# Sums of a state-space scan spread over seven slots of eight, with filler products on TensorE

## The reference

```python
def step(h, inputs):
    d_t, B_t, C_t, u_t = inputs
    dA = jnp.exp(d_t[:, :, None] * A)
    h = h * dA + (d_t * u_t)[:, :, None] * B_t[:, None, :]
    y_t = jnp.einsum('bdn,bn->bd', h, C_t)
    return (h, y_t)
...
_, ys = jax.lax.scan(step, h0, seq)
y = jnp.transpose(ys, (1, 0, 2)) + u * D
y = y * jax.nn.silu(z)
out = y @ W_out
return residual + out
```

## Time and profile before

| | |
|---|---|
| median of 3 runs | 1419.47 us (1418.7 to 1422.88) |
| profiled execution, its own time | 1428.01 us |
| its span | 1426.0 us |
| first scan starts, last scan ends | 80.7 us, 416.2 us |
| PE, DVE, ACT, POOL busy, share of the span | 78%, 60%, 37%, 40% |
| granted TensorE clock, mean over the span | 0.813 |

### The profile page before, as it was taken

How to read it: one execution, slowest core, us unless ns; L and a number is a source line. 1 busy time by engine, 2 the same in 40 slices (tenths; PEclk the granted TensorE clock), 3 DMA queues, 4 the chain that set the end, 5 groups by cost and what they waited for, 6 DMA issues and landing times. The chain is left out here.

```text
span 1426.0 us, 29397 instructions
## 1 busy us (share of the span) xinstructions
PE 1109.9 (78%) x11843; PEld 810.9 (57%) x11843; DVE 849.1 (60%) x1500; ACT 529.4 (37%) x1322; POOL 569.8 (40%) x382
## 2 busy tenths in 40 slices
PE   3478999989987989897455598599376999856795
PEld 1167888888873544555345255445365454543595
DVE  7576888888855674466512476557413486755233
ACT  2433444444332553353123163156133575612121
POOL 5079898999836503110345210010434101001332
PEclk9656888787787798999579698789578798977898
DMA  2098788777755000000273100000364000000783
GB/s 103 14 231 204 202 208 210 207 202 199 202 187 172 2 1 0 1 1 1 62 207 107 30 1 1 1 1 2 130 199 158 1 1 1 2 1 22 248 291 104
DMA packets 74229, 139.72 MB, mean 98 GB/s; under 512 B 8128, under 2 KB 28368, under 8 KB 73744
## 3 DMA queue, kind: packets, MB, share of 16 engines
q1 hardware_dynamic: 70128, 129.67, 32.2%
q0 software_dynamic: 3968, 8.18, 1.6%
HBM read 128.06 MB, written 14.82 MB: 100 GB/s over the span
## 5 line engine op out<-in xcount | busy, mean ns | idle before, releaser
L648 ACT ACTIVATE shifted_a<-scores,nmax_a 128x128 f32<-128x128 f32 x768 | 208.6, 387 | 90.9 <-DVE nmax_a L614 90.9
L1115 PE MATMUL decay<-delta,A_pairs 32*128 32x127 f32 x2048 | 183.5, 344 | 43.5 <-DVE small_pack L1209 15.9
L1190 ACT ACTIVATE decay<-decay 128x1016 f32<-128x1016 f32 x128 | 128.8, 1010 | 201.0 <-PE decay L1115 201.0
L1115 PEld LDWEIGHTS decay<-delta,A_pairs 32*128 32x128 f32 x2048 | 160.7, 243 | 64.1 <-DVE small_pack L1209 20.4
L614 DVE TENSOR_REDUCE nmax_a<-scores 128x4 f32<-128x512 f32 x192 | 123.7, 686 | 114.2 <-PE scores L553 111.9
L355 POOL TENSOR_TENSOR rstd<-ve,neghalf 128x4 f32<-128x4 f32 x30 | 31.5, 1050 | 283.9 <-DVE ve L341 283.9
L620 DVE COPY PTs_a<-PT 128x512 f32<-128x512 f32 x192 | 123.7, 682 | 3.2 <-PE PT L561 3.1
L1450 POOL DMA_INDIRECT results<-xs_s x76 | 72.9, 959 | 119.2 <-DVE xs_s L1619 108.8
L561 PE MATMUL PT<-mamba_pack,shifted_a 128*128 128x128 f32 x768 | 114.8, 295 | 3.5 <-DVE PTs_a L620 2.7
L561 PEld LDWEIGHTS PT<-mamba_pack,shifted_a 128*128 128x128 f32 x768 | 89.2, 150 | 37.5 <-issue 21.9
L1101 POOL TENSOR_TENSOR pos_bias<-pos_bias,B 128x1024 f32<-128x1024 f32 x36 | 85.2, 2383 | 10.0 <-DMA pos_bias<-du_rows 10.0
(11 more groups left out here) (391 smaller groups left out, 2192.7 us busy)
## 6 DMA issues: line engine op xcount, KB each, us to landing
pos_bias<-du_rows SPq DMA_DIRECT2D x72, 256.0 KB, 4.8
small_pack<-L3f_w SPq DMA_DIRECT2D x15, 768.0 KB
XN<-du_rows SPq DMA_DIRECT2D x38, 256.0 KB, 4.8
XNT<-du_rows SPq DMA_DIRECT2D x38, 256.0 KB, 4.8
O<-du_rows SPq DMA_DIRECT2D x36, 256.0 KB, 4.9
masked_cos<-du_rows SPq DMA_DIRECT2D x36, 256.0 KB, 4.8
masked_sin<-du_rows SPq DMA_DIRECT2D x36, 256.0 KB, 4.8
small_pack<-L2f_w SPq DMA_DIRECT2D x15, 514.0 KB
```

Of the source, the lines that this page charges most:

```text
L648: t = nc.scalar.activation(shifted[u % 4][:, j, :], scores[u % 4][:, j, :], ACT.Exp, scale=-1.0, bias=nmax[:, u % 4, j:j + 1])
L1115: t = nc.tensor.matmul(decay[k % DEEP][:, s, i, 1:S], A_pairs[strip, c, 4 * q + i, :, :].rearrange("p j n -> p (j n)"), delta[strip, c, b ...
L1190: nc.scalar.activation(x, x, ACT.Exp).then_inc(decayed, 1)
```

## The change

Only `scan_block` changes.

- The sums have seven parts (`PARTS`), in slots 8n + 11 to 8n + 17: of the 32 turns of four products, part p has those from 32p // 7 to 32(p + 1) // 7, which is 4, 5, 4, 5, 4, 5, 5 turns.
- The turning back moves to slot 8n + 19, ahead of the first part of the next unit; ScalarE's copy of the sums moves by two slots, its copy of y by two, and the placing of C by two. The first part now waits for the copy of the sums of the unit before (n >= 1), not of the one before that.
- At the end of slots 3 to 6 TensorE runs four more products, and of slot 7 eight: bf16, the 128 x 128 identity by 256 columns of `q_mask`, into the second half of the bank `YT`, which nobody reads. From slot 22 on they wait for ScalarE's last copy out of that bank (`y_copied`). There are 24 a unit; they also stand in the slots ahead of the first sums.

```diff
-    UNITS, PER, DEEP = B * IC, 8, 3
+    UNITS, PER, DEEP, PARTS = B * IC, 8, 3, 7
...
-                    if n >= 2:
-                        pe.wait_ge(sum_copied, n - 1)
-                half = part // 2
-                for turn in range(8 * (part % 2), 8 * (part % 2) + 8):
+                    if n >= 1:
+                        pe.wait_ge(sum_copied, n)
+                for turn in range(32 * part // PARTS, 32 * (part + 1) // PARTS):
+                    half = turn // 16
                     for i in range(4):
-                        token = 64 * half + 16 * i + turn
+                        token = 64 * half + 16 * i + turn % 16
                         t = nc.tensor.matmul(Y[32 * i:32 * i + 32, n % 2, half, :], Cz[:, token, :],
-                                             at_token[n % 2][:, :, token], start=(turn == 0), stop=(turn == 15))
+                                             at_token[n % 2][:, :, token], start=(turn % 16 == 0), stop=(turn % 16 == 15))
-                if part == 3:
+                if part == PARTS - 1:
                     t.then_inc(summed, 1)
...
-            for k in range(TILES + 18):
+            for k in range(TILES + 20):
                 if k < TILES:
                     multiply(k)
-                if k >= 11 and (k - 11) % 8 < 4 and (k - 11) // 8 < UNITS:
-                    gather((k - 11) // 8, (k - 11) % 8)
-                if k >= 17 and (k - 17) % 8 == 0 and (k - 17) // 8 < UNITS:
-                    turn_back((k - 17) // 8)
+                if k >= 19 and (k - 19) % 8 == 0 and (k - 19) // 8 < UNITS:
+                    turn_back((k - 19) // 8)
+                n, part = (k - 11) // 8, (k - 11) % 8
+                if 0 <= n < UNITS and part < PARTS:
+                    gather(n, part)
+                if k < TILES and (k - 19) % 8 > 2:
+                    if k > 19:
+                        pe.wait_ge(y_copied, (k - 19) // 8 + 1)
+                    for i in range(4 if part < PARTS else 8):
+                        nc.tensor.matmul(YT[:, 2:4, :], m.identb[:], m.q_mask[:, 0:2 * S], start=True, stop=True)
...
-                if k % 16 == 8 and 0 < k // 16 < B:
+                if k % 16 == 10 and 0 < k // 16 < B:
                     place_c(k // 16)
-                if k >= 15 and (k - 15) % 8 == 0 and (k - 15) // 8 < UNITS:
-                    copy_sum((k - 15) // 8)
-                if k >= 18 and (k - 18) % 8 == 0 and (k - 18) // 8 < UNITS:
-                    copy_y((k - 18) // 8)
+                if k >= 17 and (k - 17) % 8 == 0 and (k - 17) // 8 < UNITS:
+                    copy_sum((k - 17) // 8)
+                if k >= 20 and (k - 20) % 8 == 0 and (k - 20) // 8 < UNITS:
+                    copy_y((k - 20) // 8)
```

More of the change, by code:

```diff
@@ L1185, in _ @@
             place_c(0)
-            for k in range(TILES + 19):
+            for k in range(TILES + 21):
                 if k < TILES:
```

## The result

The changed kernel took 1430.02 us (median of 20 runs, 1420.27 to 1439.77), the kernel before on the same chip 1422.84 us (20 runs, 1418.4 to 1431.1). The ratio is 1.0051, 95% interval 1.0032 to 1.0069: slower by 7 us. Forecast were 1439 us and +20: the sign and the range held, the size was a third.

What follows compares the result with a forecast made beforehand. No engine full: TensorE late in some slots, idle in others, clock 0.79; changed, TensorE becomes the bound. Scan +2, end +2, half clock 16 give +20 on 1419.5: 1439 us (chance 0.5), range 1405 to 1500.

Steps and rivals of the forecast that it cites:

- the instruction stalls: In the scan, TensorE waiting for its own late instructions: 6 us taken, bounds 0 and 9.
- The half clock at the start: Scan begins at 1.2 GHz, clock rises late; with a stall or two, one and a half units at half clock, 16 us.
- the sixteen rises before: In the old scan, each clock rise followed a whole part of 64 sums, which the new order lacks.
- Rival 1: Fillers and spread sums keep TensorE at 2.4 GHz from the scan's first slots: +4, 1423 us; chance 0.22.
- The unit at full clock: Eight scan slots of TensorE work alone: 21.0 us (20.4 to 21.6), above GpSimd's 18.7, so TensorE becomes the bound.
- the changes of form: TensorE's loss when passing between kinds of products in a unit: 21 of 0.18, 3.8 us.
- rival 2: TensorE finds room in the scan, fillers falling into waits: 19.3 us a unit, 1399 us; chance 0.14.
- The new wait: Scan 8n waits until old states are summed: covered by 0.3 us thanks to fillers, otherwise some 1.3 us a unit.
- all of VectorE's waits would be for the exponentials: In the changed scan, VectorE should wait only for ScalarE's exponentials; given as a sign, without a size.
- The end: Behind the last scan: late sums about 1.4 us, later load of the constants 0.6 us more, together +2.
- the constants' load: Waits for the late sums, is issued some 1 us after the last scan's end: 0.6 us more.

Runs made afterwards that it cites:

- 0.9843 run: Changed kernel with 12 fillers a unit, all in the slot without sums, in place of 24 over five slots, start unaltered: 1406.90 us, ratio 0.9843.
- the run with 40 warming products: Changed kernel plus 40 bf16 products of 512 columns ahead of the scan and 8 fillers in each of the first eleven slots: 1440.42 us, ratio 1.0100.
- 0.9888 run: Changed kernel with 74 bf16 products ahead of the scan, more fillers in its first slots, then 12 a unit in the slot without sums: 1394.35 us, ratio 0.9888.
- the one with 74 products: Changed kernel plus 74 bf16 products ahead of the scan and 8, 8, 44, then 10 fillers a slot up to slot 10: 1412.86 us, ratio 1.0029.

## Why the prediction was right and wrong

**The step that failed is the instruction stalls**, "bounds 0 and 9, I take 6", together with "I expect it to stay there until an instruction stall". They were counted in the trace of before as if they belonged to the program's length. The runs show that they belong to the order, the clock and the traffic. Spread into parts of 32 and 40 records the sums did not stall in the changed kernel (0.4 us at most) nor with all fillers left out (0.2), and once, for 0.66 us, with fillers in the first eleven slots alone; at full clock from the start and with full DMA engines the same order did (1.50 us), and with half the traffic it did not (0.2). The reading that goes with this, not tested by itself, is that 64 records of some 28 ns in a row use up instructions faster than packets bring them while the engines are full. So the term was 0.4 and not 6, and the falls of the clock behind stalls did not come.

**The half clock at the start held**: "it rises late" was 140.4 us. The units at half clock cost (31.8 - 20.7) + (24.6 - 20.7) = 15 us over the pace at full clock; forecast 16, for "one and a half units". A unit at half clock was forecast at 31.4 and took 31.8. The agreement of 15 with 16 is in part luck: the forecast's units were to come from a late rise and from "a stall or two", and the late rise alone brought them. The reason given for it was partly wrong. The prediction read the sixteen rises before as needing a whole part of 64 sums. The changed kernel has none, and its clock rose behind the first turning back:

```profile
133.63 1.89 PE L1164 MATMUL YT<-q_mask,identb 128*128 128x256 bf16 x8
135.45 2.08 PE L1115 MATMUL decay<-delta,A_pairs 32*128 32x127 f32 x16
137.46 0.48 PE L1146 MATMUL YT<-u,D_order 128*64 128x64 f32 x2
...
138.99 1.09 PE L1132 MATMUL Y<-h,Cz 128*32 128x64 f32 x32
```

In the 0.9843 run it rose right behind 12 fillers in a row and a tile. That a busy TensorE can stay at 1.2 GHz with fillers between its tiles, as the earlier trace rows said, was borne out by the run with 40 warming products, whose first eleven slots had 8 fillers each and no gap. With 40 warming products it rose at 135.8 us behind 40 records of sums and four fillers, with neither right ahead of it. What exactly raises it stays open.

**Rival 1, the clock holds**, was right on what fillers do once the clock is up, though not from the first slots on. The Trainium skill, "TensorE: Matmul & The Clock Gate", section "Why this matters for your kernels", wants no idle gaps between bursts of products, so that the clock does not drop. The run without fillers agrees in the direction (gaps of 1.34 to 1.42 us, a fall behind each, 1.0167); the page speaks of longer gaps than these. The first 59.7 us do not agree with its advice to keep TensorE busy (58.37 us busy at 1.2 GHz).

**The unit at full clock** was 21.0 in the sum and 20.7 in the trace, inside its bounds (20.4). The mis-sized term is the changes of form, 21 of 0.18 = 3.8 us. Read from start to start, a unit is eight tiles of 1.09, seven parts of sums (three of 1.00, four of 1.23), four times four fillers in 0.54, eight in 0.97, and the turning back in 0.90, which is 20.7. By the prediction's own prices for the rest, the change is 0.24 behind a tile, 0.14 behind a part and 0.11 behind fillers, 3.5 in all. The 0.3 less a unit are -4.4 us over 14.6 units. TensorE became the bound, as forecast; rival 2 (19.3 a unit) was out.

**The new wait** of scan 8n: the estimate that without the fillers' cover TensorE would wait 1.3 us a unit was confirmed with 1.42. With them no wait of TensorE for VectorE is over 0.4 us; but that all of VectorE's waits would be for the exponentials was wrong: 47.7 us are for the sums, and cost nothing, since TensorE is late anyway.

**The end** was +2 and came as +2.0, from other parts: 1.3 us of late sums (forecast 1.4), 1.15 of a longer instruction stall, which was not in the sum, less 0.45 behind it, and nothing for the constants' load, which left 0.1 us behind the scan and took 14.4 us. That the size came out is luck.

Together, between 101.5 us and the last scan: forecast 314.7 + 2 + 16 = 332.7, measured 320.2. Of the 12.5 us, 5.6 are the stalls (6 less the 0.4 left), 4.4 the unit, 1.0 the half clock, and 1.5 are in none of these.

## What to carry over

In this scan fillers belonged where TensorE's own wait opened a gap, and nowhere else: 12 in one slot held the clock as 24 over five slots did, and the ratio went from 1.0030 to 0.9843. Count them at the price of the pace that they set, and again at half clock, where they cost double. A stall for instructions isn't a constant of a program: before counting it on, ask how fast the new order uses instructions up and how full the DMA engines are at that time, and look where the packets of the instruction queue stand. And a warm start isn't free of risk: the runs that began at full clock met a stall that half clock had hidden, and with 12 fillers their first three units took 66.1 and 66.4 us against the 65.3 of the one that began cold.

## Not expected of the hardware

- TensorE's instructions come in packets over the DMA engines, and can come late: 0.6 to 3.0 us lost near 110 us in each of the five runs at full clock with 1.06 of DMA, 0.2 at most with 0.46.
- Of stalls of about half a microsecond some stood right ahead of a fall of the clock (0.56 us at 250.0 in the run with fillers alone, 0.58 at 338.5 in the 0.9888 run; 17.1 and 6.8 us at half clock followed, with TensorE busy all the time), and others did not (0.63 and 1.05 us in the first of these runs, 0.61 and 0.66 in the one with 74 products). What tells them apart is open.
- The clock fell 2.6 us after the 40 warming products ended. At half clock, TensorE was then busy for 63.9 us on end with tiles, sums and fillers before it rose.
